# Attention loop on one Trainium2 core: VectorE's low parts placed between the two halves of a score tile's maximum

## What is computed

```python
q, k, v = (qkv[:, :, 0], qkv[:, :, 1], qkv[:, :, 2])
scale = D ** (-0.5)
scores = jnp.einsum('blhd,bmhd->bhlm', q * scale, k)
attn = jax.nn.softmax(scores, axis=-1)
o = jnp.einsum('bhlm,bmhd->blhd', attn, v).reshape(b, l, c)
return o @ W_proj + b_proj
```

## Time and profile before

| | |
|---|---|
| runs | 3148.40, 3144.75, 3148.11 us |
| median | 3148.11 us |
| profiled execution, its own time | 3139.54 us |
| its span in the profile | 3137.9 us |
| granted TensorE clock, mean over the span | 0.951 of full |
| attention's loop, first to last maximum of a head (L847) | 699.6 to 1733.0 us |

### The profile page before, as it was taken

How to read it: one execution, slowest core, us unless ns; L and a number is a source line. 1 busy time by engine, 2 the same in 40 slices (tenths; PEclk the granted TensorE clock), 3 DMA queues, 4 the chain that set the end, 5 groups by cost and what they waited for, 6 DMA issues and landing times. The chain is left out here.

```text
span 3137.9 us, 51594 instructions
## 1 busy us (share of the span) xinstructions
PE 2823.0 (90%) x16066; PEld 2289.3 (73%) x16066; DVE 1682.8 (54%) x3405; ACT 1450.7 (46%) x1863; POOL 1434.5 (46%) x1065
## 2 busy tenths in 40 slices
PE   7769999979999999999999678689999999999976
PEld 3258787846666666666666467579999999999965
DVE  4456766669998998999899355401111111111125
ACT  2122322249999999999999445511111111111112
POOL 1232323138888888888888544412222222222200
PEclk9779999979999999999999788789999999999988
DMA  6376666644334333343343357792112111111153
GB/s 202 131 262 212 234 217 218 221 116 92 85 87 94 79 92 90 84 92 86 86 93 80 127 171 219 216 320 72 37 37 72 37 37 55 54 37 38 50 163 134
DMA packets 340331, 378.73 MB, mean 121 GB/s; under 512 B 167008, under 2 KB 230120, under 8 KB 340188
## 3 DMA queue, kind: packets, MB, share of 16 engines
q1 hardware_dynamic: 330588, 357.71, 38.3%
q0 software_dynamic: 4224, 9.44, 1.7%
q10 hardware_dynamic: 5380, 9.66, 1.0%
HBM read 226.82 MB, written 158.93 MB: 123 GB/s over the span
## 5 line engine op out<-in xcount | busy, mean ns | idle before, releaser
L815 POOL TENSOR_TENSOR a_pl<-a_pf,a_ph 128x1024 fp32r<-128x1024 f32 x384 | 909.8, 2408 | 23.1 <-ACT a_pf L912 22.9
L843 DVE TENSOR_REDUCE a_mx<-a_psum_s 128x1 f32<-128x512 f32 x992 | 637.8, 684 | 92.4 <-PE a_psum_s L941 88.6
L910 ACT ACTIVATE a_ph<-a_psum_t 128x1024 fp32r<-128x1024 f32 x512 | 526.6, 1028 | 116.2 <-PE a_psum_t L958 108.9
L1562 PE MATMUL m_psum_h<-m_ht,m_w 128*128 128x256 f32 x4032 | 534.9, 284 | 30.3 <-DMA m_w<-w_s 21.0
L1514 POOL TENSOR_TENSOR m_al<-m_af,m_ah 128x256 fp32r<-128x256 f32 x288 | 212.9, 739 | 762.7 <-DVE m_ah L1523 762.7
L1523 DVE CAST m_ah<-m_af 128x256 fp32r<-128x256 f32 x288 | 84.6, 294 | 848.4 <-ACT m_af L1500 848.4
L1562 PEld LDWEIGHTS m_psum_h<-m_ht,m_w 128*128 128x128 f32 x4032 | 508.8, 189 | 34.0 <-issue 33.1
L1500 ACT ACTIVATE m_af<-m_psum_h,m_bias 128x256 f32<-128x256 f32 x288 | 137.3, 477 | 814.2 <-PE m_psum_h L1562 814.2
L1576 PE MATMUL m_psum_y<-m_w,m_ah 128*128 128x288 f32 x2304 | 504.2, 296 | 1.4 <-DVE m_y L1540 1.2
L977 PE MATMUL a_psum_o<-a_ph,a_vs 128*100 128x512 f32 x1024 | 420.0, 410 | 23.8 <-POOL a_pl L815 19.7
L978 PE MATMUL a_psum_o<-a_pl,a_vs 128*100 128x512 f32 x1024 | 404.3, 395 | 0.0
(11 more groups left out here) (225 smaller groups left out, 3106.0 us busy)
## 6 DMA issues: line engine op xcount, KB each, us to landing
a_qs<-q_s SPq DMA_DIRECT2D x192, 144.0 KB
a_ks<-k_s SPq DMA_DIRECT2D x192, 144.0 KB
w_s<-q_ws SPq DMA_DIRECT2D x64, 324.0 KB, 3.4
h_s<-p_ht SPq DMA_DIRECT2D x40, 512.0 KB, 5.1
m_ht<-h_s SPq DMA_DIRECT2D x16, 1280.0 KB, 7.8
v_s<-q_vo SPq DMA_DIRECT2D x64, 288.0 KB, 2.3
a_vs<-v_s SPq DMA_DIRECT2D x128, 144.0 KB, 4.5
q_s<-q_qko SPq DMA_DIRECT2D x32, 512.0 KB, 2.8
```

The costliest lines, as they stand in the source:

```text
L815: pool.tensor_tensor(pl[:, s % RING], pf[:, s % RING], raw(ph[:, s % RING]), ALU.subtract).then_inc(lo_pool, 1)
L843: dve.tensor_reduce(mx[:, u % 2, t, h:h + 1], p_s[:, h * 512:(h + 1) * 512], AX.X, ALU.max) \
L910: act.activation(ph[:, s % RING], p_t[:, s % 2], ACT.Exp, scale=SCALE)
L1562: m = pe.matmul(p_h[:, f % RING, 0:GM], w1[:, k, f * P:(f + 1) * P], ht[:, q, a], start=(i == 0), stop=(i == len(PASSES) - 1))
```

## The change

`max_tile`, which reduced both halves of a tile, is cut into `max_half`, which reduces one. VectorE's loop calls it twice, and the calls of `low` stand between the two. Everything that followed the second half still does; the transposition `turn` now stands behind the calls of `low`, but in its round (tile 0) there is none. All other engines' code is untouched.

```diff
-                def max_tile(hd, u, t):
-
-                    if t == 0:
+                def max_half(hd, u, t, h):
+
+                    if t == 0 and h == 0:
                         dve.wait_ge(mh_lo, hd - 1)
-                    for h in range(2):
-                        dve.wait_ge(half_ready, 2 * (KT * (hd - 2) + t) + h + 1)
-                        dve.tensor_reduce(mx[:, u % 2, t, h:h + 1], p_s[:, h * 512:(h + 1) * 512], AX.X, ALU.max) \
-                           .then_inc(half_free, 1)
-                    if t == KT - 1:
+                    dve.wait_ge(half_ready, 2 * (KT * (hd - 2) + t) + h + 1)
+                    dve.tensor_reduce(mx[:, u % 2, t, h:h + 1], p_s[:, h * 512:(h + 1) * 512], AX.X, ALU.max) \
+                       .then_inc(half_free, 1)
+                    if t == KT - 1 and h == 1:
                         dve.wait_ge(half_free, 2 + 2 * KT * (hd - 1))
                         dve.tensor_reduce(mf[:, u % 2], mx[:, u % 2], AX.X, ALU.max).then_inc(mf_ready, 1)
...
-                max_tile(2, 2, 0)
+                max_half(2, 2, 0, 0)
+                max_half(2, 2, 0, 1)
                 turn(1, 1, None)
...
                     for k in range(1, STEPS + 1):
                         over, s = divmod(k, STEPS)
-                        if not (last and u + over >= SLOTS - 2):
-                            max_tile(hd + over + 2, (u + over + 2) % SLOTS, s)
-                        if over and not (last and u >= SLOTS - 2):
-                            turn(hd + 2, (u + 2) % SLOTS, i + 1)
+
+                        ahead = not (last and u + over >= SLOTS - 2)
+                        if ahead:
+                            max_half(hd + over + 2, (u + over + 2) % SLOTS, s, 0)
                         if s + LO_AHEAD in DVE_LO and not (last and u + over == SLOTS):
                             low(hd + over, s + LO_AHEAD)
                         if s + LO_AHEAD - STEPS in DVE_LO and not (last and u == SLOTS - 1):
                             low(hd + 1, s + LO_AHEAD - STEPS)
+                        if ahead:
+                            max_half(hd + over + 2, (u + over + 2) % SLOTS, s, 1)
+                        if over and not (last and u >= SLOTS - 2):
+                            turn(hd + 2, (u + 2) % SLOTS, i + 1)
                         if (s + 1) % PER_LH == 0:
                             finish_hi(hd, s // PER_LH)
```

## The result

| | before | changed |
|---|---|---|
| median | 3146.43 us (4 runs) | 3190.69 us (3187.14 to 3195.01, 4 runs) |
| profiled execution, its own time | 3139.54 us | 3195.01 us |
| its span | 3137.9 us | 3193.4 us |
| first to last L847 (now L846) | 1033.4 us | 1087.7 us |

The ratio is 1.0143, with a 95% interval of 1.0126 to 1.0161: slower by some 45 us, where 34 were forecast with a range up to 3202. Of these, 54.2 lie in the loop over heads; what lies ahead of it (2.9 us more) and behind it (1.6 us less) nearly cancels.

What follows compares the result with a forecast made beforehand. Four engines were within a tenth of each other, meeting in the chain low part, `scores`, exponential. 18.2 us (48 heads) plus 15.5 us (14 with table load), together +34 us on the 3148.1 us median, gave 3182 us, range 3160 to 3202.

Steps and rivals of the forecast that it cites:

- The stop: TensorE, twice a head: the tile matmul waits for the late second-half reduction, so `scores` and its exponential come 0.41 us later.
- a stretched step: ScalarE's time from one exponential start to the next across a stop: 2.95 us instead of 2.54.
- The rival of a faster kernel: Only the earlier low part counts: each of 124 stops 0.41 us shorter, 51 us gained, 3097 us; chance 5%.
- The absorption: Slack in ScalarE's six other steps vanishes as TensorE is held longer: ordinary head 17.18 us, 0.38 above 16.80.
- the 0.44 us of slack: Time per ordinary head by which ScalarE's six other steps exceed 6 x 1.88 us, put down to `values` waiting for GpSimd.
- the rival in which nothing is absorbed: The six other steps keep their 0.44 us: 17.62 us an ordinary head, +61 us, 3209 us; chance 10%.
- The table load: ScalarE's reload in 14 heads adds its full 1.37 us: 18.55 us a head, 1.11 above 17.44.
- The clock: TensorE stays at full clock, granted 1.00 in a window with waits of 1.4 us; new waits about 1 us each.
- The 34 us of the sum: 48 heads without a load at 0.38 us (18.2) and 14 with one at 1.11 us (15.5).
- the upper end of the forecast's own range: `scores` slowed to 0.73 us from 0.63: each stop 0.10 us longer, 17.38 us a head, +46 us, 3194 us.
- the walk's links: Times after the exponential's end at a stop: low part 0.03, tile matmul 1.90, `scores` 2.22, next exponential 2.89 us.

Runs made afterwards that it cites:

- the late split: Kernel before, with GpSimd's split of the maxima behind the low part of step 2 instead of step 0: 3117.64 us against 3137.99, ratio 0.9939.
- step 1 alone moved: Changed kernel with the low part of step 5 put back behind both tile halves: 3176.19 us, ratio 1.0120 to the kernel before.
- the change and the late split: Changed kernel with GpSimd's split of the maxima behind the low part of step 2 instead of step 0: 3196.16 us, ratio 1.0201 to before.
- ScalarE unrolled: Changed kernel with five iterations of ScalarE's loop over heads in one, leaving 2 table loads within it: 3166.01 us, ratio 1.0087 to before.
- the late split and three rounds in one: Kernel before, with GpSimd's split of the maxima behind step 2's low part and ScalarE's loop unrolled by three: 3116.40 us, ratio 0.9922.
- step 5 alone: Changed kernel with the low part of step 1 put back behind both tile halves: 3142.71 us against 3137.32 for the kernel before, ratio 1.0018.
- scores hoisted: Changed kernel with TensorE's `scores` for steps 7 and 3 placed between the tile's two halves: 3153.77 us, ratio 1.0048 to the kernel before.

## Why the prediction was right, and where it was short

**The stop.** The main claim, that the reduction moved behind the low part would hold TensorE ahead of the very `scores` that the low part was hurried for, was right in sign, place and size: 124 waits in the changed kernel's list, a stretched step of 2.94 us for 2.95, and the experiment that lets `scores` pass brings the step to 2.12 us. The rival of a faster kernel, and with it the Trainium skill's advice (Perfetto Trace Analysis, Optimization Strategy) to make the releasing dependency start sooner, fails here for the reason given: the low part did start sooner, and was no longer what TensorE waited for.

**The absorption.** Forecast was that the 0.44 us of slack is TensorE's waits for GpSimd and would be used up: 17.18 us a head, measured 17.17. That was an argument then; the late split shows it, since it takes the slack away in the kernel before and changes no ordinary head in the changed one. It also answers the rival in which nothing is absorbed (17.62 us). Not quite all of it went: the step from 5 to 6 kept 0.08 us, and the stop for step 5 is shorter (2.91 us) than the other (2.98 us), so the two misses cancel in the head's length. The slack is also no common store, as the two kernels with one low part moved show.

**The table load.** That it would lose its cover was right: 1.11 us a head forecast, 1.09 measured.

**The clock.** The step that failed is the sentence that TensorE stays at full clock, because a window with waits of 1.4 us had shown 1.00 and the new ones would be about 1 us each. The 1.4 us are a wait of the weight loads; the matmuls' own longest wait in that window was 1.0 us, so full clock had been seen up to 1.0 us only, in the measure in which the new stand is 1.80. I had worked out the held matmul for an ordinary head and the table load for ScalarE, and never put the two together: the load holds ScalarE back ahead of the exponential for which that stop waits, while TensorE is held only 0.17 us on its way there, so its stand at that stop is 1.80 us instead of 0.84, 14 times. Behind 12 of these the clock fell and cost 18.4 us in the profiled execution. The 34 us of the sum came out as 32.6 in the loop (12.2 + 5.2 + 15.2); the missing 21.5 are these falls and the 0.22 us of a loop's turn that lost its cover as well (3.1 us). The medians are 44.3 us apart and the profiled executions 55.5, because the one stood 6.9 us below its median and the other 4.3 above; how many falls the other runs had, no profile tells.

That 3191 us came to lie between 3160 and 3202, and even under 3194, the upper end of the forecast's own range, is partly luck. That end was made of 0.20 us more in every head, for `scores` slowed after the held matmul, and nothing of the kind happened: the walk's links came out within 0.02 us and the ordinary head at 17.17 us. The room left for it was filled by falls of the clock, which the sum had at nothing.

What stays open is why a stand of 1.8 us lets the clock fall behind 12 loads and not behind the other two, behind 8 of 14 with step 1 alone moved, 14 of 14 with the change and the late split, and 1 of 2 with ScalarE unrolled, though it is as long in all four (1.8 us). Nor does length order the shorter cases: with the late split and three rounds in one, stands of 1.68 and 2.13 us were followed by a fall, and those of 1.62 and 1.71 us were not. No run here was made to tell that apart.

## What to carry to other kernels

When an operation is moved ahead of another on one engine, ask what its consumer must do first: in a queue without overtaking, hurrying what an engine waits for is worth nothing if what it must do before that has been made later by the same move. Count slack by whose wait it is before spending it; here it was one engine's stand for a small result, and moving that stand (a few lines) made the kernel 0.6% faster where the change made it 1.4% slower. And add up rare events with the common one at the place where they meet: the clock fell only behind the longest waits, which the mean of about 0.75 us (93.5 / 124) does not show.

## What was not expected of the hardware

- TensorE's clock fell to its lower level behind a single stand of 1.80 us, though heads with a load were 87% busy and the others 92%, for some 3 us, at a cost of 1.53 us each; stands of 0.3 and 0.9 us in every head never did it, and with 1.2 us behind a load it fell 10 times in 14. In the kernels whose longest stand within the loop was 1.0 us or less (before, step 5 alone, scores hoisted, late split) it never fell there.
- With a longer body, the turn of ScalarE's loop has a pause of its own beside the table load: 1.21 us of standing still ahead of the load in a body of 20 heads (1.4 and 1.9 us with the late split, 1.5 to 2.0 us in a body of 12), while a body of 4 shows none. What ScalarE waits for there, no run shows.
